# A 16-entry table lookup: GpSimd alone, or VectorE masks and GpSimd multiply and add

## The reference, cut to what matters

```python
def _ghost_linear(x, idx, lut):
    w = lut[idx]                      # lut: 16 floats
    return jnp.einsum('bsh,oh->bso', x, w)
gate = _ghost_linear(x, gate_idx, lut)      # gate_idx, up_idx: (688, 256) int32
up = _ghost_linear(x, up_idx, lut)
h = jax.nn.silu(gate) * up
return _ghost_linear(h, down_idx, lut)      # down_idx: (256, 688) int32
```

## Time and profile before

| | |
|---|---|
| median of 3 runs | 927.52 us (922.5 to 929.87) |
| the profiled execution | 930.69 us |
| its span in the profile | 928.9 us |
| mean granted TensorE clock | 0.947 of full speed |
| busy: PE, DVE, ACT, POOL | 788.6, 733.8, 575.7, 508.8 us |

### The profile page before, as it was taken

The page is one execution under the profiler, slowest core; times in us unless marked ns, Lnnn a source line. Parts: engine busy times, 40 slices in busy tenths (PEclk is TensorE's granted clock), DMA queues, the critical chain, the costliest instruction groups (busy, mean ns, idle before and its releaser), DMA issues.

```text
span 928.9 us, 17601 instructions
## 1 busy us (share of the span) xinstructions
PE 788.6 (85%) x4556; PEld 671.1 (72%) x4556; DVE 733.8 (79%) x2388; ACT 575.7 (62%) x1388; POOL 508.8 (55%) x545
## 2 busy tenths in 40 slices
PE   4768879889688898877989999988999956679998
PEld 4657658777577787765877788866888845568887
DVE  3768999899699899779989999976555678755555
ACT  3458767777566787665878789964333357433332
POOL 2599999999999999999999998100000000000000
PEclk9789999999889999888999999998999978789999
DMA  9600000000000000000000100000000000000000
GB/s 259 202 1 1 1 1 1 1 2 2 4 1 1 1 1 1 4 2 1 1 2 1 36 1 1 1 1 1 1 0 0 0 0 1 0 1 23 23 23 23
DMA packets 15393, 14.66 MB, mean 16 GB/s; under 512 B 5792, under 2 KB 14432, under 8 KB 15040
## 3 DMA queue, kind: packets, MB, share of 16 engines
q1 hardware_dynamic: 13792, 11.41, 4.2%
q0 software_dynamic: 624, 2.12, 0.7%
q10 hardware_dynamic: 880, 0.04, 0.1%
HBM read 11.46 MB, written 2.10 MB: 15 GB/s over the span
## 4 chain that ended last, share of the span: by engine, by line
PE 57%; DVE 21%; issue 14%; ACT 5%; DVEq 1%; DMA 1%; ACTq 0%; SPq 0%
PE bank L530 11%; PE bank L532 10%; PE bank L531 10%; PE bank L1280 5%; PE bank L1294 3%; DVE pt_lo L987 2%; PE bank L1297 2%; PE bank L1307 2%; PE bank L1309 2%; PE bank L1244 2%; DVE prob L978 2%; DVE bias_m L940 2%; DVE o_b L993 2%; PE bank L1255 1%; DVE q_tok L954 1%
## 5 line engine op out<-in xcount | busy, mean ns | idle before, releaser
L650 POOL TENSOR_SCALAR hot<-idx_gu,lut 128x256 f32<-128x256 bf16 x165 | 194.6, 1180 | 16.7
L700 ACT ACTIVATE prob<-bank,bias_m 128x128 f32<-128x128 f32 (+3 forms) x256 | 135.5, 529 | 49.7 <-DVE bias_m L940 48.4
L940 DVE CUSTOM_DVE_ANT_0 bank<-bank,mask 128x128 f32<-128x128 f32 (+3 forms) x256 | 126.0, 492 | 20.3 <-issue 18.5
L655 POOL TENSOR_TENSOR w_gu<-w_gu,hot 128x256 f32<-128x256 f32 x165 | 122.8, 744 | 13.8
L1280 PE MATMUL bank<-ident,prob 128*128 128x128 f32 x640 | 101.3, 282 | 22.0 <-issue 12.9
L727 ACT CAST pt_hi<-bank 128x512 fp32r<-128x512 f32 x160 | 93.7, 586 | 37.2 <-PE bank L1297 18.1
L987 DVE TENSOR_TENSOR pt_lo<-bank,pt_hi 128x512 fp32r<-128x512 f32 x160 | 108.9, 681 | 4.9 <-ACT pt_hi L727 4.6
L650 POOL TENSOR_SCALAR hot<-idx_dn,lut 128x256 f32<-128x256 bf16 (+1 forms) x90 | 98.1, 1090 | 9.1
L1280 PEld LDWEIGHTS bank<-ident,prob 128*128 128x128 f32 x640 | 75.9, 144 | 36.3 <-issue 22.0
L530 PE MATMUL bank<-kt_hi,qt_hi 128*128 128x128 f32 (+3 forms) x256 | 89.7, 351 | 10.0 <-ACT kt_hi L693 4.3
L807 ACT ACTIVATE silu<-bank 128x512 f32<-128x512 f32 x40 | 24.0, 599 | 99.0 <-PE bank L532 99.0
(11 more groups left out here) (196 smaller groups left out, 2249.1 us busy)
## 6 DMA issues: line engine op xcount, KB each, us to landing
x<-in_L_attn_a_x_dram SPq DMA_DIRECT2D x4, 512.0 KB, 7.9
wo_nat<-in_L_attn_a_wo_dram SPq DMA_DIRECT2D x1, 2048.0 KB, 12.3
out_dram<-x SPq DMA_DIRECT2D x16, 128.0 KB, 1.7
wqu<-in_L_attn_a_wq_up_dram SPq DMA_DIRECT2D x2, 768.0 KB, 7.5
wqr<-in_L_attn_a_wq_rope_dram SPq DMA_DIRECT2D x4, 192.0 KB, 7.6
raw_dn<-in_L_ffn_down_idx_dram POOLq DMA_DIRECT2D x1, 688.0 KB, 10.5
raw_gu<-in_L_ffn_gate_idx_dram POOLq DMA_DIRECT2D x1, 640.0 KB, 7.5
raw_gu<-in_L_ffn_up_idx_dram POOLq DMA_DIRECT2D x1, 640.0 KB, 8.2
```

The costliest lines, as they stand in the source:

```text
L650: nc.gpsimd.tensor_scalar(dst, idx[:, c:c + n], float(v), lut[:, v:v + 1], ALU.is_equal, ALU.mult).then_inc(lut_hot, 1)
L655: nc.gpsimd.tensor_tensor(w, w, hot[:, 0:n], ALU.add).then_inc(lut_sum, 1)
L700: nc.scalar.activation(prob[:, n % 2, h, 0:w], bank[2 + h % 2][:, 0:w], ACT.Exp, bias=bias_m[:, n % 2, h:h + 1], scale=-1.0, accum_out=den ...
L940: nc.vector.tensor_tensor_reduce(out=bank[2 + h % 2][:, 0:w], in0=bank[2 + h % 2][:, 0:w], in1=mask[:, TB * P - w:TB * P], scale=1.0, scal ...
```

## The change

The 4192 columns are laid out as one tensor `idx_all` (bfloat16) and one `w_all` (float32), and are worked in four chunks of 1048 columns. For each chunk and each v (64 pairs) VectorE writes a mask, `idx == v`, 1048 columns in bfloat16, into `one_hot`, of which there is one buffer; GpSimd multiplies it by the table value and by 1.0 into a float32 tensor (for v > 0 into the columns of the chunk behind it, as scratch) and adds that to the weights for v > 0. The masks of chunk 0 are made two at the end of each of slots 0 to 7, the others one in each slot of the loop's three passes, between `rope_q` and `qt_low` (behind L959 and in front of L964). `table_mask` waits until the multiply of the mask before has ended (lut_hot); GpSimd's multiply waits for its mask (lut_mask). All F tasks now wait for all 60 adds. `hot` goes.

```diff
+CHUNKS = 4
-        idx_gu = keep("idx_gu", [P, GT, DIM], BF16)
-        idx_dn = keep("idx_dn", [P, CK, INTER], BF16)
-        w_gu = keep("w_gu", [P, GT, DIM], F32)
-        w_dn = keep("w_dn", [P, CK * INTER], F32)
+        NGU, NW = GT * DIM, GT * DIM + CK * INTER
+        CH = NW // CHUNKS
+        w_at = keep.at
+        w_all = keep("w_all", [P, NW], F32)
+        w_room = nc.alloc_sbuf_tensor_at("w_room", [P, NW + CH], F32, offset=w_at)
+        idx_all = keep("idx_all", [P, NW], BF16)
+        one_hot = keep("one_hot", [P, CH], BF16)
...
-        F_TASKS = [(lut_sum, gu_sums, t_gu(c, k), (3 + 3 * c + k) % 8) for c in range(CK) for k in range(3)]
-        F_TASKS += [(lut_sum, gu_sums + dn_sums, t_dn(k), (9 + k) % 8) for k in range(3)]
+        F_TASKS = [(lut_sum, (LUT - 1) * CHUNKS, t_gu(c, k), (3 + 3 * c + k) % 8) for c in range(CK) for k in range(3)]
+        F_TASKS += [(lut_sum, (LUT - 1) * CHUNKS, t_dn(k), (9 + k) % 8) for k in range(3)]
...
-                for c in range(0, cols, GC):
-                    n = min(GC, cols - c)
-                    w = w_flat[:, c:c + n]
-                    for v in range(LUT):
-                        dst = hot[:, 0:n] if v else w
-                        nc.gpsimd.tensor_scalar(dst, idx[:, c:c + n], float(v), lut[:, v:v + 1],
-                                                ALU.is_equal, ALU.mult).then_inc(lut_hot, 1)
-                        n_hot += 1
-                        pool.wait_ge(lut_hot, n_hot)
-                        if v:
-                            nc.gpsimd.tensor_tensor(w, w, hot[:, 0:n], ALU.add).then_inc(lut_sum, 1)
-                            n_sum += 1
-                            pool.wait_ge(lut_sum, n_sum)
+            for c in range(CHUNKS):
+                w = w_room[:, c * CH:(c + 1) * CH]
+                spare = w_room[:, (c + 1) * CH:(c + 2) * CH]
+                for v in range(LUT):
+                    n = c * LUT + v
+                    pool.wait_ge(lut_mask, n + 1)
+                    nc.gpsimd.tensor_scalar(spare if v else w, one_hot[:, :], lut[:, v:v + 1], 1.0,
+                                            ALU.mult, ALU.mult).then_inc(lut_hot, 1)
+                    if v:
+                        pool.wait_ge(lut_hot, n + 1)
+                        nc.gpsimd.tensor_tensor(w, w, spare, ALU.add).then_inc(lut_sum, 1)
+                        pool.wait_ge(lut_sum, c * (LUT - 1) + v)
...
+            def table_mask(c, v):
+
+                free_after(dve, lut_hot, c * LUT + v)
+                nc.vector.tensor_scalar(one_hot[:, :], idx_all[:, bass.ds(c * CH, CH)], float(v), None, ALU.is_equal)\
+                    .then_inc(lut_mask, 1)
 
             def dve_slot(s, b, nb, early=(0, 0)):
...
                 if s < 2:
                     dve_tasks(dve, *early)
+                if nb is not None:
+                    table_mask(b + 1, s - LEAD)
                 between(10)
                 do(qt_low, s - 1)
...
             for s in range(LEAD):
                 dve_slot(s, 0, None, early_tasks(s))
+                if s == 0:
+                    dve.wait_ge(idx_ready, 2)
+                for v in (2 * s, 2 * s + 1):
+                    table_mask(0, v)
```

More of the change, by code:

```diff
@@ L88, in build @@
         x = keep("x", [P, BATCH * TB, DIM], F32)
-        idx_gu = keep("idx_gu", [P, GT, DIM], BF16)
-        idx_dn = keep("idx_dn", [P, CK, INTER], BF16)
-        w_gu = keep("w_gu", [P, GT, DIM], F32)
-        w_dn = keep("w_dn", [P, CK * INTER], F32)
-        raw_gu = nc.alloc_sbuf_tensor_at("raw_gu", [P, GT, DIM], I32, offset=keep.at - 4 * (GT * DIM + CK * INTER))
-        raw_dn = nc.alloc_sbuf_tensor_at("raw_dn", [P, CK, INTER], I32, offset=keep.at - 4 * CK * INTER)
+        NGU, NW = GT * DIM, GT * DIM + CK * INTER
+        CH = NW // CHUNKS
+        w_at = keep.at
+        w_all = keep("w_all", [P, NW], F32)
+        raw_all = nc.alloc_sbuf_tensor_at("raw_all", [P, NW], I32, offset=w_at)
+        w_room = nc.alloc_sbuf_tensor_at("w_room", [P, NW + CH], F32, offset=w_at)
+        idx_all = keep("idx_all", [P, NW], BF16)
+        one_hot = keep("one_hot", [P, CH], BF16)
+        raw_gu = raw_all[:, 0:NGU].rearrange("p (t d) -> p t d", t=GT)
+        raw_dn = raw_all[:, NGU:NW].rearrange("p (c f) -> p c f", c=CK)
+        w_gu = w_all[:, 0:NGU].rearrange("p (t d) -> p t d", t=GT)
+        w_dn = w_all[:, NGU:NW]
         down_hi = keep("down_hi", [P, CK, DOWN], F32R)
@@ L189, in build @@
         wo_t = nc.alloc_sbuf_tensor_at("wo_t", [P, HEADS, DIM], F32, offset=late_at)
-        GC = GT * DIM // 11
-        hot = r2("hot", [P, GC], F32)
-        GU_CHUNKS, DN_CHUNKS = GT * DIM // GC, -(-CK * INTER // GC)
         bank = [nc.alloc_psum_tensor(f"bank{i}", [P, 512], F32) for i in range(8)]
@@ L211, in build @@
         qu_dup, qr_dup, v_dup = sem("qu_dup"), sem("qr_dup"), sem("v_dup")
-        lut_hot, lut_sum = sem("lut_hot"), sem("lut_sum")
+        lut_mask, lut_hot, lut_sum = sem("lut_mask"), sem("lut_hot"), sem("lut_sum")
         prep_mm, prep_act, prep_dve = sem("prep_mm"), sem("prep_act"), sem("prep_dve")
@@ L635, in _ @@
             pool.wait_ge(gu_in, 64)
-            nc.gpsimd.tensor_copy(idx_gu[:, :, :], raw_gu[:, :, :]).then_inc(idx_ready, 1)
+            nc.gpsimd.tensor_copy(idx_all[:, 0:NGU], raw_all[:, 0:NGU]).then_inc(idx_ready, 1)
             pool.wait_ge(dn_in, 16)
-            nc.gpsimd.tensor_copy(idx_dn[:, :, :], raw_dn[:, :, :]).then_inc(idx_ready, 1)
+            nc.gpsimd.tensor_copy(idx_all[:, NGU:NW], raw_all[:, NGU:NW]).then_inc(idx_ready, 1)
             pool.wait_ge(idx_ready, 2)
[L640 to L644, removed]
-                for c in range(0, cols, GC):
-                    n = min(GC, cols - c)
-                    w = w_flat[:, c:c + n]
-                    for v in range(LUT):
-                        dst = hot[:, 0:n] if v else w
-                        nc.gpsimd.tensor_scalar(dst, idx[:, c:c + n], float(v), lut[:, v:v + 1],
-                                                ALU.is_equal, ALU.mult).then_inc(lut_hot, 1)
-                        n_hot += 1
-                        pool.wait_ge(lut_hot, n_hot)
-                        if v:
-                            nc.gpsimd.tensor_tensor(w, w, hot[:, 0:n], ALU.add).then_inc(lut_sum, 1)
-                            n_sum += 1
-                            pool.wait_ge(lut_sum, n_sum)
+            for c in range(CHUNKS):
[10 more added lines that the diff above has]
+                        pool.wait_ge(lut_sum, c * (LUT - 1) + v)
         @block.scalar
```

2 lines of the change are left out of this document (removed).

## The result

| | before | after | forecast |
|---|---|---|---|
| median | 925.4 us (922.5 to 929.87) | 961.1 us (957.8 to 963.68) | 968 (927 to 1035) |
| ratio to before | 1 | 1.0357, 95% interval 1.0323 to 1.0391 | 1.044 |
| profiled execution, span | 930.69, 928.9 us | 963.68, 961.5 us | 971.7 |

The account below looks back on a forecast made before the run. VectorE's order of work was taken to set the pace in the attention, with GpSimd's work beside it. Loop +12, first slots +33 and last batch -4 gave +41 on the 927.5 us median: 968 us, range 927 to 1035.

Parts of the forecast that it names:

- The lead: Slots 0 to 7: paired masks wait for the buffer, and GpSimd's adds hold VectorE; +33 us.
- The prices: Per 1048-column instruction: GpSimd multiply 1.1 us, add 2.44 us; VectorE mask 0.49 us, of which 0.42 after overlap.
- Rival 1: GpSimd's multiply is as slow as its comparison, 3.87 us: 1032 us in all; chance 0.21.
- Rival 2: GpSimd's multiply takes 2.3 to 3.4 us, so the add's end reaches L978: 996 us; chance 0.08.
- Rival 4: VectorE's masks run by columns, 0.78 us each, 18 us more: 986 us; chance 0.08.
- Rival 3: GpSimd's long add doesn't hold VectorE to its end: +3 us, 931 us in all; chance 0.16.
- The loop: Three passes: masks 20, waits 4 and 11, less 18, make 17 us more on VectorE; 5 vanish in gaps: +12.
- present waits: VectorE's waits for GpSimd in the kernel before (L978, L959, small steps); 18 us of them go in the loop.
- new waits: VectorE held by the longer adds in the loop: 4 us in short slots, 11 in slots 8 and 10.
- long slots: Loop slots with 4.98 us from L964 to the next L978, against 3.25 in short ones; they meet no hold.
- The last batch: GpSimd is done by then, so twelve slots lose waits of 0.3 us each: -4 us.
- the case of a holding multiply: If a GpSimd multiply held the shared port pair too, the sum would be some 3 us higher.

Follow-up runs that it names:

- one a slot: The changed kernel with one mask in each slot from slot 0 on, none doubled, the last 8 in the last batch: 931.5 us, 1.005 of the kernel before.
- short adds: The changed kernel with GpSimd's adds on 8 of the 1048 columns, masks and multiplies whole: 929.9 us, 1.003 of the kernel before.
- long kernel of GpSimd alone: The changed kernel without VectorE masks; GpSimd compares and multiplies itself, 1048 columns at a time: 980.2 us, 1.060 of the kernel before.
- both short: The changed kernel with GpSimd's multiplies and adds on 8 columns each, masks whole: 911.1 us, 0.982 of the kernel before.
- all split: The kernel of one a slot with split adds, with each multiply in four pieces too: 932.7 us, 1.005 of the kernel before.
- one a slot with split adds: The changed kernel with one mask in every slot and each add in four pieces of 262 columns: 920.7 us, 0.991 of the kernel before.

## Why the prediction was right, and where it wasn't

**The sum, +41 forecast, +32.6 in the profiled executions: nearer than its parts.** The three stages of the forecast gave +28.8 (29.8 - 0.3 - 0.7); the rest came from the preparation, +7.2, which I had at 0, less 3.3 behind the attention. That the total lies so near the forecast is partly luck.

**The lead, +33 forecast, +29.8 measured: right by its mechanism.** Each step is in the timeline: the second mask waits for the multiply (1.34), then the L973 pair and L954 are held by one add each. With the adds short 12.2 us go, with the masks one a slot all but 0.9. By the ends of the `rope_q` adds, counted from the lead's start, slot 0's pair cost 0.3 us (forecast 1.5), the pairs of slots 0 to 2 together 9.0 (forecast 10.5) and slots 3 to 7 the other 20.8 (24). What I had not counted is that the multiply holds the L973 as well; it is a part of why short adds gave back 12.2 us in the lead and not 23.

**The prices: multiply and add right,** to 5%; **the mask too dear,** 0.426 us recorded against 0.49, and 0.34 against 0.42 of added busy time. Rivals 1, 2 and 4 fell with them. The rule that I weighed for the mask, of the Trainium skill ("VectorE: DVE Perf Modes", the perf-mode tier table), four 16-bit columns a cycle, agrees: from 8 to 1048 columns the mask grew by 0.26 us, 0.25 ns a column, where `normalise` on 32-bit data has 0.55.

**Rival 3, the add lets go early: wrong.** L954 waited to 0.15 us before the end of the add, as in the earlier trace rows with an add a third as long, and the long kernel of GpSimd alone lost 52 us by length alone.

**The loop, +12 forecast, -0.3 measured: the step that failed is the present waits.** "Against that the present waits go: ... 18" should have read 35. By the groups in the loop, before against both short, `normalise` had 14.8 us of wait where I took 10 (I had only the 512-column form's excess over the whole run, 583 - 482 ns; in the loop it is 617, and the other forms have as much or more), L959 5.5 (I took 5), and the small steps of layer norm and token steps some 15 where I took 3. One form of `normalise` and one token step, in the loop of the kernel before, then that `normalise` with both short:

```profile
L978 DVE TENSOR_SCALAR prob<-prob,rden 128x384 f32<-128x384 f32 x24 | 13.0, 571 | 0.0
...
L904 DVE TENSOR_SCALAR cd<-cd,rms_r 128x192 f32<-128x192 f32 x12 | 5.1, 448 | 0.0
```
```profile
L973 DVE TENSOR_SCALAR prob<-prob,rden 128x384 f32<-128x384 f32 x24 | 9.1, 413 | 0.0
```

The new waits were mis-sized too, 23 us against 4 + 11 = 15, and in the same place: L899 in the loop, 448 ns before (L904) and 306 with both short, rose to 786. The groups after, of the loop alone:

```profile
L954 DVE TENSOR_TENSOR q_tok<-q_tok,q_rot 128x256 f32<-128x256 f32 x48 | 20.4, 425 | 1.7
L973 DVE TENSOR_SCALAR prob<-prob,rden 128x512 f32<-128x512 f32 x24 | 10.5, 481 | 0.0
L973 DVE TENSOR_SCALAR prob<-prob,rden 128x128 f32<-128x128 f32 x24 | 9.7, 444 | 0.0
...
L899 DVE TENSOR_SCALAR cd<-cd,rms_r 128x192 f32<-128x192 f32 x12 | 9.2, 786 | 0.0
```

L954 and the long L973 are free of GpSimd, as forecast for the long slots. So VectorE's sum is +17 for masks (I had 20), +23 and -35, that is +5 (393.8 to 399.1) where I had +17. Its idle time fell by 5.6 us (45.8 to 40.2), as I had let it (5), though I had counted the gaps in a window of 124 us that is not a whole pass: a pass takes 143.7 to 149.6 us.

**The last batch, -4 forecast, -0.7 measured.** VectorE's busy time there fell by 1.0: the kernel before had lost hardly anything in these slots.

**The preparation and the rest,** +7.2 and -3.3, have no step in the forecast. The rest varies by nearly as much among kernels that don't differ in it: 301.3 us in all split, 303.9 in one a slot with split adds.

**"The tensor_scalar of GpSimd mostly doesn't [hold]": wrong for the multiply,** right only in part for the comparison. I had given the case of a holding multiply 3 us, and short adds against both short puts its waits in the loop at 380.6 - 376.1 = 4.5. The rule of the Trainium skill ("SBUF — State Buffer", "Who interferes with whom"), that the two engines share a pair of ports and that whoever starts first keeps it for the whole instruction, agrees with the add, the multiply and the casts here, to 0.1 to 0.2 us of their ends; it doesn't with the comparison.

## What to carry to other kernels

Work that is off the critical path is not free when it holds something: price it by the length of its single instruction and by where in the other engine's order it falls, not by its busy time (GpSimd's 508.8 us cost VectorE 35 us of waits in the loop; its 233.7 us cost 23 there and, by way of pairs of masks, 24 of the lead's 29.8). Measure the waits that a change removes as carefully as those it adds: cut the suspect instruction to 8 columns, and the other engine's busy time tells them at once, if overlaps between neighbouring instructions are counted once. Put such work where the other engine has a stretch that doesn't need the port, one piece a slot, split where it can't be avoided, and check that its last piece still ends inside that stretch.

## What the runs showed of the hardware that I had not expected

GpSimd's comparison holds VectorE in two stretches and leaves it free between them. In long, GpSimd alone, the first row pair is a `rope_q` add (L953, 0.42 us by itself) that starts 0.55 us into a comparison, the second one that starts 3.09 into it; then a `normalise` pair (L972, 0.41 each) at 2.34 and 2.86:

```profile
416.37 3.82 POOL L647 TENSOR_SCALAR w_room<-idx_all,lut 128x1048 f32<-128x1048 bf16 x1
416.92 0.86 DVE L953 TENSOR_TENSOR q_tok<-q_tok,q_rot 128x256 f32<-128x256 f32 x1
...
301.87 3.93 POOL L647 TENSOR_SCALAR w_room<-idx_all,lut 128x1048 f32<-128x1048 bf16 x1
...
304.96 0.43 DVE L953 TENSOR_TENSOR q_tok<-q_tok,q_rot 128x256 f32<-128x256 f32 x1
...
148.92 3.83 POOL L647 TENSOR_SCALAR w_room<-idx_all,lut 128x1048 f32<-128x1048 bf16 x1
151.26 0.41 DVE L972 TENSOR_SCALAR prob<-prob,rden 128x384 f32<-128x384 f32 x1
151.78 1.18 DVE L972 TENSOR_SCALAR prob<-prob,rden 128x384 f32<-128x384 f32 x1
```

The first waits until 0.99 us behind the comparison's start (416.92 + 0.86 - 0.42 = 417.36); three others that start at 0.46, 0.69 and 0.82 wait to the same 0.99, and none of those that start later waits. `normalise` goes through at 2.34 and is held from 2.86 to 3.63, 0.2 before the comparison's end; of the seven adds of `rope_q` that start from 2.88 to 3.57 none is held. In the kernel before, with 256 columns, the early stretch ends at 0.32, which is why show an L959 go through at 0.33; another (at 471.20, 0.07 behind its comparison) took 0.67 us. That the early stretch is GpSimd's reading and the late one its writing, and that only `normalise` needs the second, would fit; no run takes the two apart.

The other surprise is that a hold belongs to one instruction. Four adds of 262 columns in a row, without a pause that GpSimd's own row would show, let a waiting VectorE instruction in between two of them. Splitting costs GpSimd 0.45 us an add: the four overlap by 0.04 us each, and all 60 adds take 175.1 us instead of 148.3.
